# Row maxima carried to the heads' rows by DMA through DRAM instead of by TensorE, and x for the statistics fetched ahead of the output's weights

## The reference, cut to what matters

```python
qkv = t @ w_qkv + b_qkv
q, k, v = jnp.split(qkv, 3, axis=-1)
scores = jnp.einsum('bhnd,bhmd->bhnm', q, k) / jnp.sqrt(jnp.float32(hd))
attn = jax.nn.softmax(scores, axis=-1)
out = jnp.einsum('bhnm,bhmd->bhnd', attn, v)
out = out @ w_o + b_o
# x + logmap0(mhsa(expmap0(x * m))) + mhsa(x * (1 - m)), all in float32
```

## Time and profile before

| | us |
|---|---|
| median of 3 runs | 4022.13 (4021.23 to 4025.07) |
| the profiled execution | 4021.88 |
| its span in the profile | 4020.2 |
| PE busy | 3937.1 (98%), 21664 matmuls |
| POOL busy | 2664.2 (66%) |
| DVE busy | 2345.5 (58%) |
| ACT busy | 1928.7 (48%) |
| chain that ended last | PE 94%, DVE 2%, POOL, DMA, ACT 1% each |
| DMA | 293.12 MB, mean 73 GB/s |

### The profile page before, as it was taken

The page is one execution under the profiler, slowest core; times in us unless marked ns, Lnnn a source line. Parts: engine busy times, 40 slices in busy tenths (PEclk is TensorE's granted clock), DMA queues, the critical chain, the costliest instruction groups (busy, mean ns, idle before and its releaser), DMA issues.

```text
span 4020.2 us, 57048 instructions
## 1 busy us (share of the span) xinstructions
PE 3937.1 (98%) x21664; PEld 2379.5 (59%) x21664; DVE 2345.5 (58%) x2553; ACT 1928.7 (48%) x3489; POOL 2664.2 (66%) x1303
## 2 busy tenths in 40 slices
PE   4999999999999999999999999999999999999998
PEld 3556566565655656556565665656556565565654
DVE  5464755647556475565746557465674656646455
ACT  4454534545345453555535545354553545535443
POOL 4584875838667486674857658675685756858468
PEclk9999999999999999999999999999999999999999
DMA  8212031121311213112141120411113121121101
GB/s 277 100 42 95 32 116 58 43 95 32 124 50 48 95 32 126 53 48 90 32 135 49 48 79 32 142 48 68 53 47 127 48 74 48 56 96 44 58 11 64
DMA packets 137548, 293.12 MB, mean 73 GB/s; under 512 B 16704, under 2 KB 28992, under 8 KB 127296
## 3 DMA queue, kind: packets, MB, share of 16 engines
q1 hardware_dynamic: 137280, 289.47, 21.2%
HBM read 239.09 MB, written 50.33 MB: 72 GB/s over the span
## 4 chain that ended last, share of the span: by engine, by line
PE 94%; DVE 2%; POOL 1%; DMA 1%; issue 1%; ACT 1%; SPq 0%; POOLq 0%; DVEq 0%; ACTq 0%
PE aux_ps L1310 32%; PE acc_ps L1422 23%; PE score_ps L1408 22%; PE aux_ps L1359 8%; PE score_ps L1310 4%; PE aux_ps L1432 3%; DVE mxp L1173 1%; PE aux_ps L1369 1%; POOL sums L673 1%; DMA w_split<-v_y 0%; DMA w_split<-w_o 0%; DMA xin<-in_x_dram 0%; PE aux_ps L1328 0%; PE aux_ps L1325 0%; POOL w_o L653 0%
## 5 line engine op out<-in xcount | busy, mean ns | idle before, releaser
L673 POOL TENSOR_TENSOR sums<-sums,probs 128x1024 f32<-128x1024 f32 x768 | 1835.4, 2390 | 736.9 <-ACT probs L850 682.6
L1173 DVE TENSOR_REDUCE mxp<-aux_ps 128x2 f32<-128x1024 f32 x1014 | 1241.7, 1225 | 1299.9 <-PE aux_ps L1359 1291.5
L850 ACT ACTIVATE probs<-score_ps 128x512 f32<-128x512 f32 x2048 | 1058.1, 602 | 658.7 <-PE score_ps L1408 648.0
L1422 PE MATMUL acc_ps<-probs,v_y 128*64 128x512 f32 x4096 | 991.9, 605 | 0.0
L1310 PE MATMUL aux_ps<-xs,w_qk 128*128 128x512 f32 x2976 | 804.7, 408 | 0.0
L1310 PEld LDWEIGHTS aux_ps<-xs,w_qk 128*128 128x128 f32 x2976 | 524.8, 188 | 374.3 <-issue 279.1
L673 POOL TENSOR_TENSOR sums<-probs 128x1024 f32<-128x1024 f32 x128 | 305.0, 2383 | 432.8 <-ACT probs L850 432.1
L1422 PEld LDWEIGHTS acc_ps<-probs,v_y 128*64 128x64 f32 x4096 | 248.2, 136 | 475.2 <-issue 245.2
L1359 PE MATMUL aux_ps<-k_hi,q_hi 64*128 64x512 f32 x2028 | 454.0, 443 | 18.7 <-DVE mxp L1173 16.1
L1235 DVE RECIPROCAL den<-den 128x256 f32<-128x256 f32 (+1 forms) x240 | 443.4, 1848 | 17.3 <-ACT den L861 17.3
L1408 PE MATMUL score_ps<-q_hi,k_hi 64*128 64x512 f32 x2048 | 407.9, 393 | 1.0 <-issue 1.0
(11 more groups left out here) (142 smaller groups left out, 3195.2 us busy)
## 6 DMA issues: line engine op xcount, KB each, us to landing
w_qk<-w_split SPq DMA_DIRECT2D x124, 512.0 KB, 4.2
xin<-in_x_dram SPq DMA_DIRECT2D x232, 256.0 KB, 3.3
w_o<-w_split SPq DMA_DIRECT2D x32, 1024.0 KB, 7.3
w_v<-w_split SPq DMA_DIRECT2D x30, 1024.0 KB, 5.9
v_y<-in_x_dram SPq DMA_DIRECT2D x72, 256.0 KB, 3.0
y<-v_y SPq DMA_DIRECT2D x64, 256.0 KB, 2.0
xin<-y SPq DMA_DIRECT2D x64, 256.0 KB, 2.9
out_dram<-v_y SPq DMA_DIRECT2D x64, 256.0 KB, 6.5
```

The costliest lines, as they stand in the source:

```text
L673: pool.tensor_tensor(sums[h][:, :], a, probs[:, g % SLOTS_P, :], ALU.add).then_inc(c_sum[h].sem, 1)
L850: act.activation(probs[:, n % SLOTS_P, token_half(u % 2)], score_ps[:, u % SCORE_BANKS, :], ACT.Exp, scale=SCALE).then_inc(c_exp.sem, 1)
L1173: dve.tensor_reduce(mxp[:, :, n, h], ps, AX.X, ALU.max).then_inc(c_free["D"].sem, 1)
L1422: last = nc.tensor.matmul(acc_ps[head(j), :], v_y[:, m, head(2 * p + j)], probs[:, n % SLOTS_P, token_half(j)], start=(m == 0), stop=(m == ...
```

## The change

The turn of the maxima no longer uses PE and the identity. `combine` runs in two halves, after slots 11 and 15 (batches `8p-3` and `8p-1`), each with a wait for the DMA that read its buffer last. ACT issues, at the end of its own batch turns, a DMA that stores each half of `mxw` to DRAM (`store_neg`, batches `8p-3` and `8p-1`) and one that loads it from there into rows 0 and 64 of `q_max` (`load_neg`, batches `8p-2` and `8p`; the second half of pair 4 in batch 0 of the next stage). The store has 1024 elements of 4 bytes, which lie 128 to a row in DRAM while in SBUF a partition holds 8 of them; the load has two rows of 512 elements. `load_neg` waits on ACT for its store. PE waits for the load at the first tile of each half. In SP's program the loads of `w_o` go behind the x chunks for statistics (stage 0) or for the norm (stage 1).

```diff
+HALF_DONE = (11, 15)
+NEG_STORE, NEG_LOAD = (-3, -1), (-2, 0)
+def neg_at(b, what):
+    for h in range(2):
+        p, r = divmod(b - what[h], 8)
+        if r == 0 and 1 <= p <= PAIRS:
+            return p, h
+    return None
...
+        max_dram = nc.dram_tensor("row_maxima", (2, 2, HALF), F32, kind="Internal").ap()
-        mxw = sb("mxw", [P, HD + NT], F32R)
+        mxw = sb("mxw", [P, 2, 2, NT // 2], F32R)
-        ident = sb("ident", [P, P], F32R)
...
(SP)
-                    load_wide(w_o, t, 6, c_wo)
                     if t == 0 and followed(i):
                         load_chunks(i, 0, "stats", range(8), next_image)
                         load_gate(i, 0)
                     if t and followed(i):
                         load_chunks(i, 1, "norm", range(4, 8), next_image)
+                    load_wide(w_o, t, 6, c_wo)
...
(ACT)
-            def neg_rows(i, t, p):
-                for h in range(2):
-                    ps = aux_made(act, i, (t, "neg", p, h))
-                    act.activation(q_max[0:HD + 1, p % 2, token_half(h)], ps[0:HD + 1, :],
-                                   ACT.Copy).then_inc(c_free["A"].sem, 1)
+            def store_neg(i, t, p, h):
+                n = 0 if i is None else 4 * t + p
+                act.wait_ge(c_mx.sem, c_mx.at(i, h + 1 if i is None else 2 * (n - 1) + h + 1))
+                if i is not None:
+                    act.wait_ge(c_neg[h].sem, c_neg[h].at(i, 16 * (n - 1)))
+                act.dma_start(max_dram[h].rearrange("j (n q) -> q (j n)", q=P),
+                              mxw[:, h, :, :].bitcast(F32).rearrange("p j n -> p (j n)")).then_inc(c_mst[h].sem, 16)
+            def load_neg(i, t, p, h):
+                act.wait_ge(c_mst[h].sem, c_mst[h].at(i, 16 if i is None else 16 * (4 * t + p)))
+                last = TILES * t + 16 * (p - 2) + 8 * h + 8
+                if i is not None and (i or last > 0):
+                    act.wait_ge(c_score.sem, c_score.at(i, 2 * last))
+                act.dma_start(q_max[0:HD + 1:HD, p % 2, token_half(h)].bitcast(F32), max_dram[h]).then_inc(c_neg[h].sem, 16)
...
+                    if (p, k) == (PAIRS + 1, 2):
+                        store_neg(None, -1, PAIRS, 0)
-            neg_rows(None, -1, PAIRS)
+            load_neg(None, -1, PAIRS, 0)
+            store_neg(None, -1, PAIRS, 1)
+            load_neg(None, -1, PAIRS, 1)
...
+                    def neg_turn(b):
+                        if b == 0 and t:
+                            load_neg(i, 0, PAIRS, 1)
+                        elif b == 0 and i:
+                            load_neg(i - 1, 1, PAIRS, 1)
+                        elif neg_at(b, NEG_LOAD) and wanted(i, t, neg_at(b, NEG_LOAD)[0]):
+                            load_neg(i, t, *neg_at(b, NEG_LOAD))
+                        if neg_at(b, NEG_STORE) and wanted(i, t, neg_at(b, NEG_STORE)[0]):
+                            store_neg(i, t, *neg_at(b, NEG_STORE))
...
                         operand_step(i, t, b)
+                        neg_turn(b)
...
(DVE)
-            def combine(i, t, p):
-                aux_read(dve, i, (t, "max", p, 15))
-                for j in range(2):
-                    dve.tensor_reduce(mxw[:, HD * j:HD * j + NT], mxp[:, j, :, :], AX.X, ALU.max,
-                                      negate=True).then_inc(c_mx.sem, 1)
+            def combine(i, t, p, h):
+                aux_read(dve, i, (t, "max", p, HALF_DONE[h]))
+                if i is not None:
+                    dve.wait_ge(c_mst[h].sem, c_mst[h].at(i, 16 * (4 * t + p - 1)))
+                dve.tensor_reduce(mxw[:, h, :, :], mxp[:, :, 4 * h:4 * h + 4, :], AX.X, ALU.max,
+                                  negate=True).then_inc(c_mx.sem, 1)
...
(PE)
-            def neg_rows(i, t, p):
-                pe.wait_ge(c_mx.sem, c_mx.at(i, 2 if t < 0 else 2 * (4 * t + p)))
-                for h in range(2):
-                    ps = bank_free(pe, i, (t, "neg", p, h))
-                    for n in range(4):
-                        last = nc.tensor.matmul(ps[0:HD + 1, n * P:(n + 1) * P], mxw[:, 4 * h + n:4 * h + n + HD + 1],
-                                                ident[:, :], start=True, stop=True)
-                    last.then_inc(c_aux.sem, 1)
...
-                            if p:
-                                aux_read(pe, i, (t, "neg", p, 1))
-                            elif t:
-                                aux_read(pe, i, (0, "neg", PAIRS, 1))
-                            else:
-                                pe.wait_ge(c_free["A"].sem, c_free["A"].at(i, 0))
+                        if m == 0:
+                            pe.wait_ge(c_neg[h].sem, c_neg[h].at(i, 16 * (4 * t + p)))
```

More of the change, by code:

```diff
@@ L166, in maxima @@
         return [((t, "max", p, s), "D", (0, 1))]
-    def neg(p):
-        return [((t, "neg", p, h), "A", (h,)) for h in range(2)]
     if t < 0:
-        p = PAIRS
         out = [((t, g), "D", (0,)) for g in GATES]
@@ L179, in aux_tiles @@
                 out += [((t, what, pp, k), "D", (first, first + 1))]
-        return out + neg(p) + maxima(p + 1, 0)
+        return out + maxima(PAIRS + 1, 0)
     out = []
@@ L187, in aux_tiles @@
             out += [((t, "den", phase_at(b, DEN)), "A", (1,))]
-        if neg_pair(b) is not None and wanted(i, t, neg_pair(b)):
-            out += neg(neg_pair(b))
         if t == 0 and b in GATE_BATCH and followed(i):
@@ L334, in build @@
         c_mx = counted("max_made", 16, 2)
+        c_mst = [counted(f"max_stored{h}", 16 * 8, 16) for h in range(2)]
+        c_neg = [counted(f"max_rows_loaded{h}", 16 * 8, 16) for h in range(2)]
         c_score = counted("scores_made", NSC)
@@ L616, in _ @@
                 sp.wait_ge(c.sem, 17 + B * 128 - 16 * PAIRS + 16)
+            for c in (*c_mst, *c_neg):
+                sp.wait_ge(c.sem, 17 + B * 128 - 16)
             sp.wait_ge(c_wv.sem, 1 + B * 64 - 32)
@@ L620, in _ @@
         def _(pool):
-            pool.memset(den[:, 0, 0:P], 0.0).then_inc(s_const, 1)
             pool.memset(group_mean[:, :], 1.0 / GROUP).then_inc(s_const, 1)
             pool.memset(ones[:, :], 1.0).then_inc(s_const, 1)
-            pool.memset(mxw[:, :].bitcast(F32), 0.0).then_inc(s_const, 1)
             pool.memset(q_max[:, :, :].bitcast(F32), 0.0).then_inc(s_const, 1)
             pool.memset(first_row[:, :].bitcast(F32), 0.0).then_inc(s_const, 1)
-            pool.wait_ge(s_const, 6)
[L628 to L634, removed]
+            pool.wait_ge(s_const, 4)
+            pool.memset(first_row[0:1, :].bitcast(F32), 1.0).then_inc(s_const, 1)
+            pool.wait_ge(s_const, 5)
+            pool.memset(first_row[HD:HD + 1, :].bitcast(F32), 1.0).then_inc(s_const, 1)
+            g3 = group_mean[:, :].rearrange("p (g c) -> p g c", c=GROUP)
+            pool.wait_ge(s_const, 6)
             pool.affine_select(out=g3, in_=g3, compare_op=ALU.is_ge, fill=0.0, base=0,
                                pattern=[[-GROUP, P // GROUP], [0, GROUP]], channel_multiplier=1).then_inc(s_const, 1)
-            pool.wait_ge(s_const, 10)
+            pool.wait_ge(s_const, 7)
             pool.affine_select(out=g3, in_=g3, compare_op=ALU.is_ge, fill=0.0, base=GROUP - 1,
@@ L890, in _ @@
                             den_copy(phase_at(b, DEN))
-                        if neg_pair(b) is not None and wanted(i, t, neg_pair(b)):
-                            neg_rows(i, t, neg_pair(b))
                         for j in HI_AT.get(b, ()):
@@ L1223, in _ @@
                     max_slot(None, -1, p, k)
-            combine(None, -1, PAIRS)
+                    if k in HALF_DONE:
+                        combine(None, -1, p, HALF_DONE.index(k))
             max_slot(None, -1, PAIRS + 1, 0)
@@ L1266, in _ @@
                                 max_slot(i, t, p, s)
[L1267 to L1268 removed]
+                                if s in HALF_DONE:
+                                    combine(i, t, p, HALF_DONE.index(s))
                             if j == 0:
```

12 lines of the change are left out of this document (2 added, 10 removed).

## The result

The changed kernel takes 4167.85 us (median of 4 runs, 4160.53 to 4178.55) against 4022.31 before: ratio 1.0363, 95% interval 1.0349 to 1.0378. It is 145 us slower. The forecast was 3992.3 (3983 to 4002), so both the sign and the size were wrong. The profiled execution has a span of 4166.9 us.

The account below looks back on a forecast made before the run. The prediction took PE to bound nearly the whole run. From 4021.88 us it took 32.3 for turns, added 4.0 at the start and took 1.6 for x: 3992.0, as median 3992.3 us, range 3983 to 4002.

Parts of the forecast that it names:

- What bounds the kernel: From 600 to 3960 us PE is the bound, busy 3345.27 of 3360 us; start and last 60 us excepted.
- What a turn costs: In the steady part, a turn on PE costs 0.47 us by distance of batch starts, 6.43 against 5.96.
- The sum of 32.3 us: Steady-part gain from removing PE's turns: 25.9 + 5.1 + 1.3 us; bounds 29.6 and 44.
- The store's landing, 3.0 us: ACT's store of 1024 4-byte pieces to DRAM lands in 3.0 us; ends 2.3 and 11.6.
- The second half "has 4 batches more": Inside the stages, the second half's store and load have 4 batches more room; all of this costed at 0.
- the rival of the late row: Slow stores stall ACT, then PE waits for q_max in 47 pairs: 122 us lost, about 4112; chance 0.06.
- S: The store's landing time in us inside stages; PE waits from 9.0, break-even with the gain near 9.7.
- The rule that speaks against it: Skill's warning against plain-DMA transposes and one descriptor per element; taken as about bulk rate, not changing the sum.
- The start: First scores near 98 instead of 94.0 us, +4.0; bounds -0.5 to +9.5; second store's wait nearly hidden.
- The third rival: At the start the first store lands with the crowd at 101, first scores at 103.5: 3998.5 us; chance 0.14.
- x ahead of `w_o`: In the first image x lands some 7 us earlier and PE's 1.57 us wait goes; reorder cost 0.
- PE's time turned into another wait: If DVE's maxima or POOL's sums nearly bound each batch, shorter batches gain nothing: 4021 us; chance 0.05.

Follow-up runs that it names:

- e4: The changed kernel with the second half's load two batches later and both stores issued straight behind their batch's exponentials: 4024.74 us, ratio 1.0006.
- e7: The changed kernel with DVE turning maxima in 32x32 blocks, 128-byte pieces stored and loaded, second load at batch 8p+2: 4002.12 us, ratio 0.9948.
- e3: The changed kernel with the second half's load two batches later, at batch 8p+2 instead of 8p: 4076.93 us, ratio 1.0136.
- e9: The changed kernel with the store's 1024 4-byte pieces written 256 bytes apart, leaving out the turn: 4013.36 us, ratio 0.9978.
- e2: The changed kernel with the store in 128 pieces of 32 bytes, leaving out the turn: 4006.31 us, ratio 0.9960.
- e1: The kernel before with only SP's reorder, `w_o` behind the x chunks, TensorE's turn kept: 4021.07 us against 4021.80, ratio 0.9998.
- e5: The kernel before plus 128 spare stores of 1024 4-byte pieces from ACT, awaited only by later stores: 4022.55 us against 4022.67, ratio 1.0000.

## Why the prediction was wrong, point by point

- **What bounds the kernel.** Right: PE. That is why nothing hid a wait once it reached PE. It cost even more than its length, since PE's granted clock was lower behind it (40 us of PE's busy time, e4).
- **What a turn costs.** The method, distance of batch starts, was right: the batch with the turn went from 6.43 to 5.98 us in e7. The sum of 32.3 us was 7 too large: 25.2 came (26.8 less 1.6). I had called the place of the first `combine` free, and had not followed PE to the stage's end, where DVE's `o_t` is next; the two are some 6.3 us of it.
- **The store's landing, 3.0 us: the step that failed.** In the kernel it was mostly 9.4 to 12 us, in the crowd of the start 14 to 18, alone 14.5. The value I took came from *reads* of 4-byte pieces, the bias loads of the earlier trace rows, and from a *large-piece* write. Each part was true: reads of small pieces are cheap (2.7 us for 1024), and so are writes of large ones. The combination of both, small writes side by side, has its own cost, and no row showed it. The step in which I called the lower end the near one, because the DMA engines are idle, argued from contention, while the cost is not contention: it is there on idle engines. The upper bound, 11.6, held most of them inside the stages; the longest was 14.3.
- **The second half "has 4 batches more": the second failure.** That holds for the data, not for ACT. The wait stood in ACT's program at batch 8p and there held the exponentials; e3 prices its place at 91 us. So the rival of the late row was the right family, but it counted one half's loss. With S = 11.6 it had 122 us for the first half, which cost 52 (e3 to e4), and nothing for the second, which cost 91, nor for the clock. That 122 lies near the sum, 143, is luck. I gave the rival 0.06. By the prediction's own bounds for S (2.3 to 11.6, decision at 9.7) that was too little, and the range should not have left it out.
- **The rule that speaks against it.** The Trainium skill, "DMA: Bandwidth & Descriptors", "Rules for kernel authors", warns of a transpose by a rearranged access pattern, and says that a non-contiguous last dimension becomes one descriptor per element. I had set both aside as being on bulk rate, which the section doesn't say. The runs side with the warning in this case: 14.5 us for 4 KB, 10 times the 1.4 us of the same bytes in 32-byte pieces. But the count of elements alone is not what costs on idle engines: spaced apart, the same count takes 3.0 us.
- **The start.** Forecast +4.0, bounds -0.5 to +9.5; it was +14.6 for the first scores and 6.7 more for the exponentials. The third rival, the store held until the crowd has landed, had the mechanism of the first store (18.1 us, and 14.2 in e9 with the pieces apart); I gave it 0.14. It put the landing at 101; the crowd itself ended 2.9 us later, and the load took 4.5 us for 2.4. The nearness of the pieces adds less there: e9's first store is 3.9 us shorter than the changed kernel's, and its first scores are 1.8 us ahead. The second store is the other way round: 14.4 us, in e9 7.9 and in e2 6.6, so the wait that I had called nearly hidden was 6.67 us, in e9 0.25.
- **x ahead of `w_o`.** The wait went as said, 1.6 us; the time of e1 is 0.7 us lower, which its interval doesn't tell from none.
- **PE's time turned into another wait.** Given 0.05 as a whole; true for a fifth of the gain.

The account: from the 4022 before, 27 us less (turns and x); the start some 23 more and one late `k_lo` 3.4 more, which gives 4022 where e4 has 4024.7; the stores' place, mainly the wait for the first half, 52 more (e3 to e4); the place of the second load 91 more (e3 to the changed kernel): 4168 from e4. The last two hold idle time and lower clock together.

## What to carry to other kernels

Price a DMA by a row that agrees in direction, in piece size and in how near the pieces lie; a read of small pieces says nothing of a write of small pieces. A wait put into an in-order engine's program is priced at the place where it stands, against what is queued behind it, not at the place where the data is needed: let the wait stand as late as the data allows. Where it reaches PE, look at the granted clock behind the pause as well as at the pause. If a transpose has to go through DRAM, write large pieces and pick the small ones in reading, or turn blocks first.

## What the runs showed of the hardware that I had not expected

- Small writes near each other in DRAM land late, on idle DMA engines: 128 pieces of 4 bytes side by side 7.4 to 8.3 us, 1024 of them 14.5 to 14.8; 1024 pieces 256 bytes apart 3.0, and in turned order 64 bytes apart 2.6 to 2.7. The share of the engines' time that the packets take does not show it (1.6% for 128 such stores).
- While 1 MB stores were landing, a 4 KB store took 14.2 us in 1024 pieces of 4 bytes, spaced apart, and 7.2 in 128 pieces of 32 bytes (e9, e2); alone 3.0 and 1.4.
- After a pause of 7.1 us PE worked at half the granted clock (0.50), and its terms of a score tile started 0.43 us apart instead of 0.23.
- The same store landed faster in the running kernel (9.4 to 12 us) than alone at the end (14.5). Why stays open.
- While such stores are under way, the median landing of bulk loads is 2 to 3 us later (w_qk 6.3 for 4.2 us, e5), although the stores move 4 KB.
- A load of 1024 pieces of 4 bytes into two partitions takes 4.7 us, 1.7 times that over 128 partitions.
